# A two-layer kernel on one core: both stages in one program per engine, and the last gate pieces placed behind the first transposes of the second stage

## What is computed

```
L0 attn: k, v, r = token-shifted mixes of x times Wk, Wv, Wr
         a running max, numerator and denominator over time (scan)
         out = sigmoid(r) * (num / den) @ Wo
L0 ffn:  y = fp8(x) @ fp8(kernel), scaled back, plus a bias, in bfloat16
L1 attn: xz = W_in x; x half: 4-tap causal convolution in time, bias, silu
         y = long convolution of x with k_ssm (by FFT), plus x * D_skip
         out = (y * silu(z)) @ W_out
L1 ffn:  a router picks the best 2 of 8 experts for each token; 2 rounds of
         hidden = gelu([x, v] w1 + b1), ctrl = hidden w2 + b2 -> alpha, beta, gate
         for the shared and the 2 chosen experts, mixed into a new x and v;
         integrated += sigmoid(halt) * refined * integration_weight
```

## Time and profile before

| what | value |
|---|---|
| device time, median of 3 runs | 466.58 us (465.35 to 467.01) |
| the profiled execution | 466.16 us, of which the span of its instructions is 464.3 us |
| PE busy | 423.1 us, 91% of the span |
| DVE busy | 330.5 us, 71% |
| ACT busy | 191.1 us, 41% |
| POOL busy | 21.7 us, 5% |
| mean granted TensorE clock | 0.964 |

### The profile page before, as it was taken

How to read it: one execution, slowest core, us unless ns; L and a number is a source line. 1 busy time by engine, 2 the same in 40 slices (tenths; PEclk the granted TensorE clock), 3 DMA queues, 4 the chain that set the end, 5 groups by cost and what they waited for, 6 DMA issues and landing times.

```text
span 464.3 us, 4188 instructions
## 1 busy us (share of the span) xinstructions
PE 423.1 (91%) x1398; PEld 211.1 (45%) x1398; DVE 330.5 (71%) x680; ACT 191.1 (41%) x314; POOL 21.7 (5%) x37
## 2 busy tenths in 40 slices
PE   4792987979969999999999999999999999999993
PEld 1241565755844465444554443433734433443361
DVE  4999899899862796497988873785553864274565
ACT  1343668543124523444325454435027525334441
POOL 0010202111010000000000000000000000000001
PEclk9896999989997999999999999999999999999997
DMA  6300000040000000000000000000000000000001
GB/s 218 148 1 0 1 1 0 2 147 0 1 2 1 1 0 0 1 1 0 1 1 0 1 0 23 0 2 0 0 0 1 23 1 1 0 0 0 1 0 45
DMA packets 5148, 7.27 MB, mean 16 GB/s; under 512 B 1075, under 2 KB 4232, under 8 KB 4872
## 3 DMA queue, kind: packets, MB, share of 16 engines
q1 hardware_dynamic: 3968, 4.80, 3.0%
q10 hardware_dynamic: 1160, 2.21, 1.3%
HBM read 5.95 MB, written 1.05 MB: 15 GB/s over the span
## 4 chain that ended last, share of the span: by engine, by line
PE 63%; DVE 3%; ACT 2%; issue 1%; POOL 0%; POOLq 0%; DVEq 0%
PE ring L1219 23%; PE ring L1197 8%; PE ring L1214 5%; PE timebank L268 4%; PE ring L1199 4%; PE specbank L256 3%; PE ring L1227 3%; PE ring L1234 2%; PE ring L1238 1%; PE ring L1241 1%; PE ring L1245 1%; PE ring L1236 1%; PE ring L1242 1%; PE ring L1210 1%; PE ring L1158 1%
## 5 line engine op out<-in xcount | busy, mean ns | idle before, releaser
L1219 PE MATMUL ring<-hm,wc 128*128 128x512 f32 (+1 forms) x252 | 108.6, 580 | 0.0
L1219 PEld LDWEIGHTS ring<-hm,wc 128*128 128x128 f32 x252 | 46.1, 190 | 61.0 <-issue 52.8
L1414 DVE SCALAR_TENSOR_TENSOR hm<-xtm,cst,h 128x512 f32<-128x512 bf16 x48 | 33.3, 745 | 6.0 <-ACT h L1325 6.0
L200 PE MATMUL bankA<-wconv,h2w 128*128 128x256 f32 x128 | 33.6, 413 | 0.0
L1339 ACT ACTIVATE gts<-ring 128x512 f32<-128x512 f32 (+1 forms) x18 | 9.9, 550 | 52.3 <-PE ring L1219 52.3
L1325 ACT ACTIVATE h<-ring,vec 128x512 f32<-128x512 f32 x32 | 21.9, 687 | 18.3 <-PE ring L1199 15.0
L200 PEld LDWEIGHTS bankA<-wconv,h2w 128*128 128x128 f32 x128 | 25.2, 205 | 5.2 <-issue 1.9
L1503 DVE SCALAR_TENSOR_TENSOR f2e<-hl,f2e 128x512 f32<-128x512 f32 (+1 forms) x9 | 5.7, 629 | 27.6 <-ACT hl L1370 27.6
L1214 PE MATMUL ring<-hm,wc 64*128 64x512 f32 (+1 forms) x84 | 22.9, 621 | 0.4 <-DVE hm L1414 0.4
L1336 ACT ACT_TABLE_LOAD x8 | 10.3, 1283 | 28.4 <-PE ring L1219 28.4
L268 PE MATMUL timebank<-cst,abc 128*128 128x256 f32 x96 | 21.2, 379 | 0.0
(11 more groups left out here) (264 smaller groups left out, 764.9 us busy)
## 6 DMA issues: line engine op xcount, KB each, us to landing
wc<-in_w_c SPq DMA_DIRECT2D x1, 1664.0 KB
cst<-in_const ACTq DMA_DIRECT2D x1, 1096.0 KB
out<-xall SPq DMA_DIRECT2D x8, 128.0 KB, 1.9
wc<-in_x_feat SPq DMA_DIRECT2D x1, 768.0 KB, 13.4
bconv<-in_bcast SPq DMA_DIRECT2D x1, 512.0 KB, 8.0
wc<-in_k_time ACTq DMA_DIRECT2D x1, 512.0 KB
wc<-in_x_feat ACTq DMA_DIRECT2D x1, 256.0 KB, 3.8
wa<-in_w_a SPq DMA_DIRECT2D x1, 256.0 KB, 3.6
```

What stands on the lines that cost most here:

```text
L200: ins = pe.matmul(at, h2w[:, n, h * P + tap:h * P + tap + P], wconv[:, tap, :], start=False, stop=(h == HALVES - 1 and tap == TAPS - 1))
L1219: ins = pe.matmul(dst[:, at], wc[:, w:w + P], hm[:, seat(j, made + g - 1), at], start=False, stop=(g == PAIRS - 1))
L1414: dve.scalar_tensor_tensor(hm[:, seat(j, k), :], picked, cst[:, C_EG + g:C_EG + g + 1], h[:, g, :], ALU.is_equal, ALU.mult).then_inc(S["hm ...
```

## The change

Both blocks become one: the functions of the first block are now called `first_sp`, `first_act`, `first_pe`, `first_pool` and `first_dve`, and the one block that is left calls them at the head of each engine's list. There is no meeting of the engines in between. With that:

- The tiles scal, half, iwh, identb and g1 lie in memory that both stages keep. Six tiles of the second stage change place, and the PSUM banks of the second stage are named in another order (ring3, ring0, specbank 0 and 1, ring1, ring2, timebank 0 and 1).
- Pieces 2 and 3 of chunk 3 move, on PE and on ACT, from the end of step c = 5 to behind `turn(0)` (`last_pieces`).
- `project_block(0)` moves on PE from behind both halves of piece 0 to between them.
- `gate(0, 0)` on DVE moves ahead of `products_now(1, 0)`, and `gate(0, 1)` to behind L300 of it, from behind L313.
- The nine settings of DVE (`scalars`) move to between `products_now(1, 0)` and `residual(0)`; ACT's tanh moves to step c = 3, behind that step's own tanh (L552) and with a wait for q_in; ACT's wait for the settings ahead of `turn(0)` is gone (the one in `spread` stays); POOL's row of g1 is set at its start, with one more wait for its own semaphore.
- SP waits for `late_split` and then copies be2split, behind its load of wc.
- `inverse(1, 0)` also waits until all pieces are kept.

```diff
@@ products_now
             s.go(dve.tensor_tensor(wide(tt[:, 0, :]), xi, taps(e, 0, 1), ALU.mult))
+            if between:
+                between()
...
                 s.link(dve.tensor_tensor(now[:, 1, :], now[:, 1, :], tt[:, 1, :], ALU.add))
-                if between:
-                    between()
-                    s.wait()
@@ first stage, act
                         act.activation(thr[:, :], psr[:, :], ACT.Tanh, scale=0.5).then_inc(kv_copied, 1)
+                        if c == CHUNKS - 1:
+                            act.wait_ge(q_in, 4 * 16)
+                            act.activation(scal[:, TSW:TSW + 1], bcs[:, B_SW:B_SW + 1], ACT.Tanh, scale=0.5).then_inc(sw_tanh, 1)
                         act.activation(der[:, DEXP:DEXP + 1], vec[:, V_TD:V_TD + 1], ACT.Exp)
...
-                    pieces(c - 2, (1, 2, 3))
+                    pieces(act, c - 2, (1, 2, 3) if c < CHUNKS + 1 else (1,))
@@ first stage, pe, c == CHUNKS + 1
                         inverse_half(pe, 0, 1, psk)
-                        piece(c - 2, 0, 0)
-                        piece(c - 2, 0, 1)
+                        piece(pe, c - 2, 0, 0)
                         pe.wait_ge(wout_in, 16)
                         project_block(pe, 0, psv)
-                        piece(c - 2, 1, 0)
-                        piece(c - 2, 1, 1)
-                        piece(c - 2, 2)
-                        piece(c - 2, 3)
+                        piece(pe, c - 2, 0, 1)
+                        piece(pe, c - 2, 1, 0)
+                        piece(pe, c - 2, 1, 1)
@@ first stage, pool
                 pool.wait_ge(columns_set, 2)
+                pool.memset(g1[RHID:RHID + 1, :], 1.0).then_inc(columns_set, 1)
+                pool.wait_ge(columns_set, 3)
@@ first stage, dve, c == CHUNKS + 1
-                        def gates():
-                            gate(dve, 0, 0, psf)
-                            gate(dve, 0, 1, psk)
-
-                        products_now(dve, 1, 0, (psr, pso), gates)
+                        gate(dve, 0, 0, psf)
+                        products_now(dve, 1, 0, (psr, pso), lambda: gate(dve, 0, 1, psk))
+                        scalars()
                         residual(dve, 0, psv)
                         long_norm(dve, 0)
                         products_late(dve, 1, 0, (psr, pso))
@@ order
                 turn(0)
+                last_pieces()
                 route_hidden(0)
@@ second stage, sp
+                first_sp(sp)
+
+                sp.wait_ge(late_split, 1)
                 sp.dma_start(be2split[HID:HID + 3 * EXPERTS, :], be2split[0:3 * EXPERTS, :]).then_inc(S["biases_doubled"], 16)
@@ second stage, pe
+                first_pe(pe)
...
+                    if c == 1 and cc == 0:
+                        pe.wait_ge(piece_kept, CHUNKS * PIECES)
                     inverse_half(pe, c, cc, Yb[cc])
...
+                def last_pieces():
+                    piece(pe, CHUNKS - 1, 2)
+                    piece(pe, CHUNKS - 1, 3)
@@ second stage, act
+                first_act(act)
...
+                def last_pieces():
+                    pieces(act, CHUNKS - 1, (2, 3))
...
-                act.activation(scal[:, TSW:TSW + 1], bcs[:, B_SW:B_SW + 1], ACT.Tanh, scale=0.5).then_inc(S["sw_tanh"], 1)
-                act.wait_ge(S["scal_set"], 1)
```

More of the change, by code:

```diff
@@ L235, in two_layers @@
         ys = sb("ys", [P, CC, TOK])
+        scal = sb("scal", [P, 6])
+        half = sb("half", [P, CTRL // P])
+        iwh = sb("iwh", [P, 2])
+        identb = sb("identb", [P, P], BF16)
+        g1 = sb("g1", [RHID + 1, TOK])
+        TSW, SW, HSW, NSW, BH2, SWDT = range(6)
         normB = [sb(f"{n}B", [P, TILES, w] if w > 1 else [P, TILES]) for n, w in (("stats", 6), ("mv", 2), ("ve", 1), ("rstd", 1))]
@@ L513, in _, with pieces, first_act @@
                 sp.dma_start(wc[:, :], w_c[:, W_RH:W_RH + W_C]).then_inc(c_in, 16)
-            @block.scalar
-            def _(act):
+            def pieces(act, c, some):
+                if valid(c):
+                    for n in some:
+                        act.wait_ge(piece_done, c * PIECES + n + 1)
+                        keep_piece(act, piecebank[n % 2][:, :], c, n).then_inc(piece_kept, 1)
+            def first_act(act):
                 act.dma_start(hT[:, :, 1:1 + WIN], x_feat[:, :, 0:WIN]).then_inc(first_in, 16)
@@ L609, in project @@
                         ins.then_inc(kvr_done, 1)
[L611 to L625, removed]
                 def turn2(c):
@@ L932, in two_layers, with order @@
             vs = lambda c: zs[:, c, 1, :]
-            Xb = [s2.enter_context(nc.psum_tensor(f"specbank{i}", [P, 512], F32)) for i in range(2)]
-            Yb = [s2.enter_context(nc.psum_tensor(f"timebank{i}", [P, 512], F32)) for i in range(2)]
-            ring = [s2.enter_context(nc.psum_tensor(f"ring{i}", [P, 512], F32)) for i in range(RING)]
+            psum = lambda name: s2.enter_context(nc.psum_tensor(name, [P, 512], F32))
+            ring3, ring0 = psum("ring3"), psum("ring0")
+            Xb = [psum(f"specbank{i}") for i in range(2)]
+            ring1, ring2 = psum("ring1"), psum("ring2")
+            Yb = [psum(f"timebank{i}") for i in range(2)]
+            ring = [ring0, ring1, ring2, ring3]
             S = {n: sem("m_" + n) for n in (
-                "scal_set sw_tanh ident_cast picked gap_ready tg_ready full kept hm_ready xn_ready "
-                "refined y_turned c_var c_rstd out_ready out_sent oh_ready biases_doubled one_set steps").split()}
+                "picked gap_ready tg_ready full kept hm_ready xn_ready "
+                "refined y_turned c_var c_rstd out_ready out_sent oh_ready biases_doubled steps").split()}
             block = s2.enter_context(nc.Block())
-            def order(turn, route_hidden, logits, spread, hidden, pair, shared, tail, forward, inverse, project_out, turn_back):
+            def order(turn, route_hidden, logits, spread, hidden, pair, shared, tail, last_pieces, forward, inverse, project_out, turn_back):
                 def hiddens(j, lo=0, hi=HU):
@@ L1075, in numbers @@
                 order(lambda c: count("turn", c), lambda c: count("route", c), lambda c: count("logits", c), spread, lambda j, e: count("hid", j, e),
-                      pair, shared, lambda j, what, half=None: count("tail", j, what, half), skip, skip, skip, skip)
+                      pair, shared, lambda j, what, half=None: count("tail", j, what, half), skip, skip, skip, skip, skip)
                 return table
@@ L1120, in _ @@
             def _(pool):
+                first_pool(pool)
                 def pow_long(c):
@@ L1277, in _ @@
                 pe.wait_ge(c_in, 4 * 16)
-                order(turn, route_hidden, logits, spread, hidden, pair, shared, tail, forward, inverse, project_out, turn_back)
+                order(turn, route_hidden, logits, spread, hidden, pair, shared, tail, last_pieces, forward, inverse, project_out, turn_back)
             @block.scalar
             def _(act):
+                first_act(act)
                 def bank(n):
@@ L1370, in tail @@
                         act.activation(hl[:, at], src[:, at], ACT.Tanh, scale=0.5, bias=scal[:, BH2:BH2 + 1]).then_inc(S["kept"], 1)
+                def last_pieces():
+                    pieces(act, CHUNKS - 1, (2, 3))
                 skip = lambda *key: None
-                act.activation(scal[:, TSW:TSW + 1], bcs[:, B_SW:B_SW + 1], ACT.Tanh, scale=0.5).then_inc(S["sw_tanh"], 1)
-                act.wait_ge(S["scal_set"], 1)
-                order(turn, route_hidden, logits, spread, hidden, pair, shared, tail, skip, skip, skip, skip)
+                order(turn, route_hidden, logits, spread, hidden, pair, shared, tail, last_pieces, skip, skip, skip, skip)
             @block.vector
             def _(dve):
+                first_dve(dve)
                 s = Steps(dve, S["steps"])
```

98 lines of the change are left out of this document (51 added, 47 removed).

## The result

The changed kernel takes 460.0 us (median of 4 runs, 459.19 to 460.52), the kernel before 466.35 on the same chip (465.35 to 467.01). The ratio is 0.9858, 95% interval 0.9844 to 0.9873. The forecast was 459.8, within 458.3 to 462.3. The profiled execution took 460.52 us around a span of 458.7.

What follows compares the result with a forecast made beforehand. PE was taken to bound the kernel, idling at the seam between the blocks and then running at half clock. -7.01 (seam) + 0.1 (x3) + 0.15 (tanh) = -6.8 us, giving 459.8 us for the median, range 458.3 to 462.3.

Steps and rivals of the forecast that it cites:

- seam after the change: PE from the end of the convolution pieces to the logits: 7.69 us after the change, 14.70 before.
- hiddens: PE's ten records of the hiddens at the seam: 4.29 us at full clock against 6.33 before, bound 4.49.
- difference at the seam: PE, convolution pieces to logits: 7.01 us less, of it 3.75 idle time and 3.26 clock.
- PE's wait for x3: PE ahead of turn(0): x3 complete at 131.95 against PE's 132.05, a tie; 0.1 us of waiting, bounds 0 and 0.7.
- ACT's tanh in step 3: The tanh moved ahead of a table load where ACT is late: costs 0.15 us, bounds 0 and 0.20.
- settings ahead of the residual: DVE's nine settings delay residual(0) by 1.1 us, from 126.4 to 127.5.
- Idle time and clock as two terms: PE at the seam loses 3.75 us idle (2.83 + 0.92) and, separately, 3.26 us through the clock at half.
- rival 1: At the seam the clock falls all the same, losing 3.26 us again: 463.1 us, chance 0.07.
- The gate pieces: Two gate pieces behind the transposes on PE take 1.98 us, up to 0.2 less since the transposes cover a wait for ACT.
- The table load: ACT's later gelu table load of 1.28 us costs nothing, hidden by PE's route and hiddens with 0.9 us to spare.
- Rival 2: Settings and gates on DVE hold back the residual, so PE waits 1.8 us for x3: 461.5 us, chance 0.07.
- Rivals 3 and 4: 3: clock falls and x3 late, or seam's wait not the limit, 464.7, chance 0.04; 4: clock stays low long, slower, 0.03.

Runs made afterwards that it cites:

- e1_fill_before: Kernel before, with matmuls whose results nobody reads in PE's two pauses at the seam, the meeting of engines kept: 464.16 us, ratio 0.9955.
- e2_gap: Changed kernel with PE waiting, ahead of the first transposes, for four powers of a waste tile on POOL (2.62 us idle): 463.02 us, ratio 0.9936.
- e7_two_pauses: Changed kernel with six POOL powers to wait for and the gate pieces back ahead of the first transposes, no meeting of engines: 466.19 us, ratio 1.0003.
- e3_pieces_back: Changed kernel with the last two gate pieces back ahead of the first transposes on PE and ACT: 461.22 us, ratio 0.9888.
- e4_order_back: Changed kernel with project_block(0) back behind both halves of piece 0 on PE and both gates back in their old place on DVE: 461.1 us, ratio 0.9886.
- e8_merge_alone: Changed kernel with gate pieces, project_block(0) and gates back in their old order and DVE's settings behind products_late: 460.88 us, ratio 0.9879.
- e6_gap_long: Changed kernel with PE waiting, ahead of the first transposes, for seven powers of a waste tile on POOL (6.22 us idle): 468.44 us, ratio 1.0048.

## Why the prediction was right

Step by step, with the prediction's terms on the left:

| term | forecast | measured |
|---|---|---|
| seam after the change | 7.69 us | 7.78 by the chain, as forecast (7.71 by the timeline) |
| of it transposes and two gate pieces | 0.44 + 1.98 | 2.32 by the chain (133.32 to 135.64) |
| route | 0.98 | 0.97 |
| hiddens | 4.29, bound 4.49 | 4.49 |
| difference at the seam | 7.01 | 6.92 |
| PE's wait for x3 | 0.1 | 0 |
| ACT's tanh in step 3 | 0.15 | 0.09 |
| settings ahead of the residual | 1.1 | 0.77 |
| time | 459.8 | 460.0 |

- **Idle time and clock as two terms** held: e1_fill_before took the clock's part alone, e2_gap paid idle time alone, and e7_two_pauses paid both and came back to the kernel before. The clock's term was somewhat too large, 3.26 against the 2.70 of e1_fill_before. In the sum that is hidden: of the rest, 0.28 us (transposes) came all the same, once PE no longer waited for ACT, and 0.1 came from the gate pieces.
- **What brought the clock down** was read wrongly. The prediction says that the clock fell behind the two pauses, and in rival 1 that only two pauses close together brought it down. The trace of the kernel before, in finer stretches, has it fall at about 137.25, between the two: behind the pause of 2.83 us, 0.4 us into the transposes, and ahead of the pause of 0.92, which is at half throughout.

```profile
137.00:137.25 0.25, 0.25 (x4) 0.25 (x3) 0.25 (x3) 0.00 (x0) 0.19 (x1) 1.00 0.00 0
137.25:137.50 0.25, 0.25 (x3) 0.00 (x0) 0.18 (x6) 0.00 (x0) 0.00 (x0) 0.52 0.00 0
137.58:138.50 0.92, 0.00 (x1) 0.00 (x0) 0.24 (x4) 0.63 (x2) 0.00 (x0) 0.50 0.08 20
```

  In e7_two_pauses it also fell ahead of the second pause, at about 138.5 where that pause starts near 139.3. So the meeting's own pause was enough, with at most the transposes behind it, and no sum depended on the other. Whether e1_fill_before needed its filler in the second pause was not tried. Because the change takes that pause away, the forecast of a full clock held.
- **The gate pieces** were 0.1 us shorter, by the wait for ACT's copy of piece 1 that the transposes now cover: their four records take 1.72 us of the chain, against 1.83 in e3_pieces_back, where they stand ahead of the transposes. The prediction had up to 0.2 as a bound. The hiddens were longer by 0.2, also a bound.
- **x3** was a tie in the forecast and came 0.45 us early. The settings cost 0.77 us because the first three, which took 0.64 us from the start of the first to the start of the fourth at the block's beginning, take 0.38 inside a running program; the residual also starts 0.07 us before the last of them ends. The forecast took their price from the only row there was, at the seam, and that row holds some of the seam's own cost, 0.26 us by these two figures.
- **The tanh**: from the start of L552's tanh to the table load it is 0.62 us before (70.95 to 71.57) and 0.71 after (70.61 to 71.32). It overlaps its neighbour by half.
- **The table load** cost nothing, as forecast by the trace. The timeline of ACT after:

```profile
135.67 0.60 ACT L211 ACTIVATE zs<-bankA 128x512 f32<-128x512 f32 x1 [0.26 <-PE bankA L204]
136.29 1.28 ACT L1320 ACT_TABLE_LOAD   x1
137.58 0.68 ACT L1320 ACTIVATE g<-ring,vec 32x512 f32<-32x512 f32 x1
```

  g starts 1.29 us after the load starts. The drain of about 1.38 us that the Trainium skill adds ("ScalarE: Activation LUTs", What ACT_TABLE_LOAD costs) is not there; by it, an estimate, g would have started near 139.0, and PE shows no wait for it.
- **Rival 1** (the clock falls all the same) asked for the clock to be at 0.50 from 137.5; it read 1.00. Nor did the waits of 0.67 to 0.74 us that e3_pieces_back, e4_order_back and e8_merge_alone have around the transposes bring it down. The Trainium skill's sentence that transposes do not count as work for the clock ("TensorE: Matmul & The Clock Gate", Part 4) had no effect that these runs show: the transposes are 0.4 us between other work.
- **Rival 2** (x3 late) is what e4_order_back makes of the kernel, at 0.67 us rather than 1.8. The order that the change brings is what kept it away.
- **Rivals 3 and 4** did not come. That the time came within 0.2 us is in part luck: the forecast started from a median of 466.58 that one more run brought to 466.35, and took off 6.8 where 6.35 came in that comparison and 6.9 in the next (466.91 to 460.01). It also went from span to median by one added 0.4 us and did not know that PE's arrival at the seam shifts by up to 1.3 us from one profile to the next.

## What to carry to other kernels

A meeting of all engines costs PE twice: the idle time, and then half of PE's pace for several us; here 3.75 us and about 3 us. Merging the two blocks won 6.0 us of the two together, and the new order the wait of 0.74 us that was left. When a step is moved out of one pause to fill another, read what it was covering: here the moved gate pieces would have uncovered x3 by 0.7 us, and the moved product covered it again. A pause on PE is worth closing, by real work first and by useless matmuls if there is none, only where PE bounds the stretch behind it: at 96 us it gave 1 us, at 76 us nothing.

## What the runs showed of the hardware that was not expected

- One pause of 2.62 us behind more than 20 us of steady work left the clock full (e2_gap). At the same place one of 2.83 (the kernel before), one of 3.32 (e7_two_pauses) and one of 6.22 us (e6_gap_long) brought it to half. A shorter one, of 2.39 us at 76 us in the kernel before, is followed by half clock as well, 1.1 us after PE has begun to work again:

```profile
78.13 0.38 PE L196 MATMUL bankA<-rowsplit,cstb 3*128 3x512 bf16 x1 [2.39 <-ACT h2w L571]
```
```profile
78.13:79.25 1.12, 1.12 (x5) 0.81 (x6) 1.03 (x3) 1.12 (x4) 0.00 (x0) 0.99 0.00 0
79.50:82.50 3.00, 3.00 (x10) 2.41 (x9) 2.96 (x3) 0.11 (x1) 0.00 (x0) 0.50 0.03 5
```

  Every profile in which that pause was not filled shows this, and in ten of them two pauses of 1.24 and 1.36 us with 0.66 us of transposes between them did it at 96 us. The length of a single pause does not decide alone. What else does was not tried further.
- In kernels that are all but the same up to that point, the fall at 96 us showed in the mean clock of 94 to 104 us as 0.83 in five profiles and as 0.66 in five. Of the two profiles compared above, it makes some 1.3 us of difference at the seam, a fifth of what this change gained.
- The crossing itself has a price apart from the waiting. In the kernel before, PE's first instruction starts 0.48 us after DVE's last one ends (136.38 to 136.86), and in e1_fill_before, where PE had worked until 0.8 us before, the same 0.48 (137.06 to 137.54).
